# A gated delta-rule step: keys and queries against the state in one group, the squares summed on VectorE, and the Gram groups apart

## The reference

```
q = silu(conv(x @ Wq));  k, v likewise      # causal convolution over 4 tokens, w[0..3]
beta = sigmoid(x @ Wb)
q, k = l2norm(q), l2norm(k)                 # per head
M = I + strictly_lower(beta * k k^T);  u = M^-1 (beta v);  w = M^-1 (beta k)
for each chunk:   u = u - w S
                  o = q S + lower(q k^T) u
                  S = S + k^T u
x2 = x + layernorm(rmsnorm(o) @ Wo);  h = layernorm(x2)
out = x2 + layernorm(experts(h) + shared(h))    # router: 4 of 32 experts; shared: silu-gated pair of products
```

## Time and profile before

| | us |
|---|---|
| median of three runs | 1088.2 (1084.99, 1088.2, 1091.24) |
| the profiled execution | 1077.42, its span 1075.7 |
| busy in the span: PE, DVE, ACT | 862.9, 659.8, 340.2 |
| mean granted TensorE clock | 0.912 of full speed |

### The profile page before, as it was taken

One profiled execution on the slowest core, in us unless ns is written; L12 is line 12 of the kernel. 1 busy time (PEld: TensorE's weight loads), 2 busy tenths in 40 slices (PEclk: granted clock), 3 DMA queues, 4 the chain that ended last, 5 costly groups with the idle time before them and its releaser, 6 DMA issues. The chain is left out here.

```text
span 1075.7 us, 35367 instructions
## 1 busy us (share of the span) xinstructions
PE 862.9 (80%) x15631; PEld 655.3 (61%) x15632; DVE 659.8 (61%) x1251; ACT 340.2 (32%) x635; POOL 118.3 (11%) x187
## 2 busy tenths in 40 slices
PE   6585697898889999979988998388783899999900
PEld 5565666666567676656766767156452777887800
DVE  2788498688579778968967986943238122222226
ACT  2423423532443352343353344122321122122205
POOL 2000000000000000000000000000001445444244
PEclk9886698999899999999999999789896899999965
DMA  8110002005100200200200110020106699999768
GB/s 276 63 41 3 4 2 82 5 2 198 68 5 13 91 4 3 101 4 3 80 24 3 37 46 4 1 81 4 59 20 235 240 360 361 356 353 351 257 139 241
DMA packets 48641, 113.42 MB, mean 105 GB/s; under 512 B 8576, under 2 KB 8704, under 8 KB 48368
## 3 DMA queue, kind: packets, MB, share of 16 engines
q1 hardware_dynamic: 42224, 96.50, 24.7%
q0 software_dynamic: 6272, 14.68, 6.3%
HBM read 84.34 MB, written 26.84 MB: 103 GB/s over the span
## 5 line engine op out<-in xcount | busy, mean ns | idle before, releaser
L465 PE MATMUL bank<-xnT,wring 128*128 128x256 f32 x768 | 170.0, 382 | 0.0
L465 PEld LDWEIGHTS bank<-xnT,wring 128*128 128x128 f32 x768 | 145.6, 191 | 23.6 <-issue 4.2
L1575 PEld LDWEIGHTS ps_g<-xgT,wring 128*128 128x128 f32 x1024 | 120.8, 194 | 17.2 <-issue 17.2
L1575 PE MATMUL ps_g<-xgT,wring 128*128 128x128 f32 x1024 | 121.2, 277 | 1.3 <-ACT xgT L1605 1.3
L1708 DVE TENSOR_TENSOR hid<-ps_g,sg 128x160 f32<-128x160 f32 x32 | 10.4, 325 | 147.9 <-ACT sg L1615 147.9
L993 DVE SCALAR_TENSOR_TENSOR cv<-pre,taps,cv 128x1024 f32<-128x1024 f32 x72 | 92.4, 1283 | 2.1
L1484 POOL MEMSET xgT<- 128x512 f32 x2 | 1.0, 532 | 796.7 <-POOLq L1786 796.7
L608 PE MATMUL bank<-hT,sg_w 128*128 128x256 f32 x256 | 72.4, 410 | 0.0
L608 PE MATMUL bank<-hT,su_w 128*128 128x256 f32 x256 | 67.3, 399 | 0.0
L618 PE MATMUL bank<-sd_w,sh_h 128*128 128x512 f32 x128 | 66.5, 643 | 0.9 <-DVEq L1114 0.9
L1605 ACT ACTIVATE xgT<-ps_x 128x320 f32<-128x320 f32 x32 | 14.0, 437 | 160.0 <-PE ps_x L1564 160.0
(11 more groups left out here) (192 smaller groups left out, 1488.8 us busy)
## 6 DMA issues: line engine op xcount, KB each, us to landing
wring<-in_ffn_W_gate SPq DMA_DIRECT2D x32, 512.0 KB, 10.2
wring<-in_ffn_W_up SPq DMA_DIRECT2D x32, 512.0 KB, 11.1
wring<-in_ffn_W_down SPq DMA_DIRECT2D x32, 512.0 KB, 11.7
x_in<-in_attn_x SPq DMA_DIRECT2D x8, 512.0 KB, 3.5
x_res<-in_attn_x SPq DMA_DIRECT2D x8, 512.0 KB, 4.3
x_rows<-x SPq DMA_DIRECT2D x8, 512.0 KB, 2.8
h_rows<-h SPq DMA_DIRECT2D x8, 512.0 KB, 3.8
side_rows<-acc_sb SPq DMA_DIRECT2D x8, 512.0 KB, 6.0
```

The lines of the kernel that those rows point to most:

```text
L465: m = te.matmul(bank[:, c * COLS:(c + 1) * COLS], wqkv[:, w, kt, ct * P:(ct + 1) * P], xnT[:, kt, :], start=(kt == 0), stop=(kt == KT - 1))
L1575: m = te.matmul(ps_g[q % 2][:, (2 * a + i) * P:(2 * a + i + 1) * P], w[:, k, i * P:(i + 1) * P], xgT[q % 2][:, k, :], start=(k == 0), stop ...
```

## The change

Seven things are done at once:

- `core` multiplies the state with keys and queries in one group of 32 matmuls, each 32x64, into one bank (`ps_c[j % 2]`). The state is now the stationary operand, so the keys' product comes out turned, and `residual` turns it back with a transpose before it subtracts. The other products of a chunk go to the other bank, and the banks change roles from chunk to chunk. A chunk has four groups and four fillers.
- `output_squares` no longer multiplies q's squares by a second matrix. VectorE adds them, scaled, to the output's squares (`output_sums`), and four of eight matmuls a step remain.
- ScalarE's `take_projection` writes a second result, the bank times the last tap, into the convolution's output. VectorE's convolution starts from it with three taps.
- `turn_h` comes after the whole projection, and `take_h` after all of `take_projection`. The router moves into the first filler of the core.
- One Y moves a filler later, and so do E and D pieces.
- `gram` is split: groups 0 and 1 come between pieces of the up-projection ahead of the squares, 2 and 3 behind them; `take_x` comes ahead of `gate_factor`, and the ring's order has X ahead of F.
- On VectorE `scale_output` comes ahead of `turn_k` and `turn_v`, and `route_experts` stands between the two halves of `hidden`.

```diff
-ORDER = dict(... two="PHEFXIOGW", loop="PHVYEFXIOGW", ...)
+ORDER = dict(... two="PHEXFIOGW", loop="PHVYEXFIOGW", ...)
...
-    ps_ws, ps_o = banks[6], banks[7]
+    ps_c = banks[6:8]
...
-                    if n == 4 and phase not in ("begin", "one"):
-                        turn_h(s - 2, phase)
-            if phase not in ("begin", "one"):
-                router(s - 2, s + 1)
...
-                now = state[j % 2]
+                now, here, aside = state[j % 2], ps_c[j % 2], ps_c[(j + 1) % 2]
...
-                        m = te.matmul(ps_ws[quad(hh), i * DK:(i + 1) * DK], kq[quad(hh), i * J + j, 0, :], now[quad(hh), i, :], start=True, stop=True)
+                        m = te.matmul(here[quad(hh), i * 64:(i + 1) * 64], now[quad(hh), i, :], kq[quad(hh), i * J + j, :, :].rearrange("p a c -> p (a c)"),
+                                      start=(i == 0), stop=False, skip_group_check=True)
                 m.then_inc(ks_done, 1)
-                fill(5 * j)
...
+                fill(4 * j)
...
-                for i in range(I8):
-                    for hh in range(HT):
-                        te.matmul(ps_o[quad(hh), i * CH:(i + 1) * CH], now[quad(hh), i, :], kq[quad(hh), i * J + j, 1, :],
-                                  start=(i == 0), stop=False, skip_group_check=True)
-                fill(5 * j + 1)
...
+                if not (isinstance(s, int) and s == 0 and j == 0):
+                    pe.wait_ge(o_out, J * s + j)
+                    pe.sem_inc(pe_passed, 1)
                 pe.wait_ge(resid_ready, J * s + j + 1)
...
-            pe.wait_ge(qsq_ready, s + 1)
-            pe.wait_ge(osq_ready, s + 1)
+            pe.wait_ge(sums_ready, s + 1)
...
-                    te.matmul(bank[:, c * COLS:(c + 1) * COLS], headsq[:, :], q_sq[:, cols], start=True, stop=False)
-                    m = te.matmul(bank[:, c * COLS:(c + 1) * COLS], headsm[:, :], o_r[:, cols], start=False, stop=True)
+                    m = te.matmul(bank[:, c * COLS:(c + 1) * COLS], headsm[:, :], o_r[:, cols], start=True, stop=True)
...
-        FILL = ["VVVV", "Y", "Y", "Y", "Y", "E", "E", "E", "E", "", "D", "D", "D", "D", "F", "F", "F", "", "F", ""]
+        FILL = ["VVRVV", "Y", "Y", "Y", "YE", "E", "E", "E", "DD", "D", "D", "F", "F", "F", "F", ""]
...
         def body(s, phase):
             project(s, phase)
+            if phase != "one":
+                turn_h(s - 2, phase)
...
+            up(0)
+            up(1)
+            gram(s, phase, (0,))
+            up(2)
+            gram(s, phase, (1,))
+            up(3)
             output_squares(s - 1, phase)
-            if phase != "one":
-                for q in range(2, 4):
-                    shared_up(s - 2, phase, "F", 1, q)
-            gram(s, phase)
+            gram(s, phase, (2, 3))
             out_proj(s - 1, phase)
...
-                link(sc_e.activation(pre[:, w, 4 * half:4 * half + 4, HALO:], ring.bank(first, n)[:, :].rearrange("p (i t) -> p i t", t=TT), ACT.Copy))
+                bank = ring.bank(first, n)[:, :].rearrange("p (i t) -> p i t", t=TT)
+                sc_e.activation(pre[:, w, 4 * half:4 * half + 4, HALO:], bank, ACT.Copy)
+                link(sc_e.activation(cv[:, w, 4 * half:4 * half + 4, :], bank, ACT.Copy, scale=taps[:, w, TAPS - 1:TAPS]))
...
             take_projection(s, phase, 1, 0)
-            take_projection(s, phase, 2, 2, (0,))
+            take_projection(s, phase, 2, 2)
             if phase != "one":
                 take_h(s - 2, phase)
-            take_projection(s, phase, 2, 2, (1,))
-            if phase != "one":
                 take_scores(s - 2)
...
-            link(v.tensor_scalar(cv[:, w, :, :], pre[:, w, :, 0:TT], taps[:, w, 0:1], None, ALU.mult))
-            tap(w, 1)
+            tap(w, 0)
         def conv_end(w, s):
+            tap(w, 1)
             tap(w, 2)
-            tap(w, 3)
...
-            v.tensor_tensor(resid[:, :, :], ps_ws[:, 0:256].rearrange("p (i d) -> p i d", d=DK), v_tok[:, :, :].rearrange("p (i j) d -> p j i d", j=J)[:, j], ALU.subtract).then_inc(resid_ready, 1)
+            link(v.transpose(resid[:, :, :], ps_c[j % 2][:, :].rearrange("p (i a c) -> p i a c", a=2, c=CH)[:, :, 0, :]))
+            v.tensor_tensor(resid[:, :, :], resid[:, :, :], v_tok[:, :, :].rearrange("p (i j) d -> p j i d", j=J)[:, j], ALU.subtract).then_inc(resid_ready, 1)
...
+        def output_sums(s):
+            dve.wait_ge(qsq_ready, s + 1)
+            dve.wait_ge(osq_ready, s + 1)
+            v.scalar_tensor_tensor(out=o_r[:, :], in0=q_sq[:, :], scalar=RMS_EPS * DK * DK, in1=o_r[:, :], op0=ALU.mult, op1=ALU.add).then_inc(sums_ready, 1)
...
             silu_kq(1, 0, s)
+            output_sums(s - 1)
+            if phase != "one":
+                hidden_gate(s - 2, phase, 1)
+                route_experts(s - 2)
+                hidden_up(s - 2, phase, 1)
+            scale_output(s - 1)
             turn_k()
-            if phase != "one":
-                route_experts(s - 2)
             turn_v()
-            if phase != "one":
-                hidden(s - 2, phase, 1)
-            scale_output(s - 1)
             masks(s, phase)
```

More of the change, by code:

```diff
@@ L62 @@
 LAG = dict(P=0, G=0, X=-1, O=1, W=1, H=2, E=2, F=2, I=2, V=3, Y=3)
-ORDER = dict(begin="XPGX", one="PXOGW", two="PHEFXIOGW", loop="PHVYEFXIOGW", seven="PHVYEFIOGW", end="HVYEFIOWVYHEFIVY")
+ORDER = dict(begin="XPGX", one="PXOGW", two="PHEXFIOGW", loop="PHVYEXFIOGW", seven="PHVYEFIOGW", end="HVYEFIOWVYHEFIVY")
 LOOP_FROM, LOOP_TO = 3, STEPS - 1
@@ L239, in step_part @@
     sig_ready = [sem(f"sig_ready{n}") for n in range(3)]
-    act_ready = [sem(f"act_ready{n}") for n in range(3)]
+    v_turned = sem("v_turned")
     halo_done = sem("halo_done")
@@ L467, in project, with gram @@
                     m.then_inc(ring.full(first, n), 1)
-                    if n == 4 and phase not in ("begin", "one"):
-                        turn_h(s - 2, phase)
-            if phase not in ("begin", "one"):
-                router(s - 2, s + 1)
-        def gram(s, phase):
+        def gram(s, phase, columns=range(J)):
             first, st = where(phase, "G", s)
             pe.wait_ge(kq_ready, 2 * (s + 1))
-            for j in range(J):
+            for j in columns:
                 ring.wait_free(pe, first, st, j)
@@ L524, in core @@
                     for hh in range(HT):
-                        m = te.matmul(ps_ws[quad(hh), i * DK:(i + 1) * DK], invT[quad(hh), i * J + j, :], resid[quad(hh), i, :], start=True, stop=True)
+                        m = te.matmul(aside[quad(hh), i * DK:(i + 1) * DK], invT[quad(hh), i * J + j, :], resid[quad(hh), i, :], start=True, stop=True)
                 m.then_inc(solved, 1)
-                fill(5 * j + 2)
+                fill(4 * j + 1)
                 pe.wait_ge(unew_ready, J * s + j + 1)
@@ L532, in core @@
                     for hh in range(HT):
-                        m = te.matmul(ps_ws[quad(hh), i * DK:(i + 1) * DK], k_tok[quad(hh), i * J + j, :], unew[quad(hh), i, :], start=True, stop=True)
+                        m = te.matmul(aside[quad(hh), i * DK:(i + 1) * DK], k_tok[quad(hh), i * J + j, :], unew[quad(hh), i, :], start=True, stop=True)
                 m.then_inc(ds_done, 1)
-                fill(5 * j + 3)
+                fill(4 * j + 2)
                 pe.sem_inc(pe_passed, 1)
@@ L638, in fill @@
                 for c in FILL[n]:
+                    if c == "R":
+                        router(s - 2, STEPS if phase == "end" else s + 1)
+                        continue
                     at = done[c]
@@ L641, in fill @@
                     if c in "VY":
-                        if phase != "two" and not (phase == "end" and c == "V"):
+                        if phase != "two":
                             shared_down(s - 3, phase, "VY".index(c), at)
@@ L672, in _ @@
         turn_h(STEPS - 2, "end")
-        for ft in range(FT):
-            shared_down(STEPS - 3, "end", 0, ft)
-        router(STEPS - 2, STEPS)
         core(STEPS - 1, "end", filler(STEPS, "end"), STEPS, STEPS - 1)
-        for q in range(2):
+        for q in range(4):
             shared_up(STEPS - 2, "end", "F", 1, q)
         output_squares(STEPS - 1, "end")
-        for q in range(2, 4):
-            shared_up(STEPS - 2, "end", "F", 1, q)
         out_proj(STEPS - 1, "end")
@@ L1299, in _ @@
         route_experts(STEPS - 2)
+        output_sums(STEPS - 1)
         hidden(STEPS - 2, "end", 1)
```

54 lines of the change are left out of this document (27 added, 27 removed).

## The result

| | before | after |
|---|---|---|
| median of the timed runs, us | 1087.6 (1084.99 to 1091.24) | 1101.2 (1096.54 to 1102.49) |
| ratio, 95% interval | | 1.0131 (1.0100 to 1.0163) |
| span of the profiled execution | 1075.7 | 1099.5 |
| mean granted TensorE clock | 0.912 | 0.897 |

The change makes the kernel 1.3% slower. I had forecast 1086, no difference; the time lies at the upper end of the range and at rival 2 (1098). The profiled execution of before lies 1% under its median and that of after at its median, so the two spans overstate the difference (24 us against 14). I use them for where the time goes.

What follows compares the result with a forecast made beforehand. TensorE hardly rests and its instruction stream also limits it, with VectorE's slack 2.3 us. Terms over the eight steps sum to -8.4 us; +6 for the clock leaves -2.4, given as 1086 us against 1088.2, range 1072 to 1102.

Steps and rivals of the forecast that it cites:

- rival 2: Slower: turn_k and turn_v ahead of the masks delay h by 4.0 us, clock falls every step; about 1098, chance 0.24.
- The front: From turn_x's transposes to chunk 0's inverse product: 55.3 us, 2.1 later than now, on ScalarE's path by a hair.
- The core: From chunk 0's inverse product to the next step's turn_x: 33.0 us against 35.95 now.
- The late Y: In the core, the last Y behind the next chunk's group makes unew late: 2.0 us lost, with 0.4 before it.
- The clock's price: TensorE's granted clock falls after idle holes in about half of the steps: +6 us, bounds nothing to 15.
- The wide group: In each core chunk, one 32x64 group of 0.91 us replaces two of 0.68: 0.45 us saved a chunk.
- The issue stalls: TensorE stalls among small matmuls, some 127 pairs apart: fewer expected after the change, 1 us left in the core.
- The first core: The core without filler: 28.9 us at 960 instead of 1152 records, -5.5 us, above its chain of some 23.
- The sums: Query squares added on VectorE: output_sums costs 1.28 us there, TensorE saves four matmuls, 1.7 us a step.
- The stream: Dense small matmuls are limited to 3.8 to 4.2 us per 127 pairs; the core loses a fifth of its instructions.
- rival 3: Issue stalls don't depend on the number of instructions, or are hidden; about 1105, chance 0.04.
- the last: Last core, free of sigmoids: -5.4 us, with its front +3.7, together -1.7.

Runs made afterwards that it cites:

- e2: The changed kernel with the last tap as a VectorE multiply again and one ScalarE pass; ratio 1.0180 to the kernel before.
- e1: The changed kernel with VectorE's turn_k and turn_v ahead of scale_output again; ratio 1.0023 to the kernel before.
- e5: The changed kernel with the last Y moved back into chunk 0, behind its first filler; ratio 1.0057 to the kernel before.
- e4: The kernel before with only the one 32x64 group, the banks' roles and the residual's transpose; ratio 0.9740 to the kernel before.
- e3: The kernel before with only the squares' sums on VectorE, ahead of turn_k, and four matmuls fewer a step; ratio 1.0134.
- e12: The changed kernel with the query squares multiplied on TensorE again and output_sums gone; ratio 1.0306 to the kernel before.

## Why the prediction was wrong

**The front** was rightly read, and a little short. scale_output came at +12.0 (said +11.6), the inverse at +19.35 (+18.4), h at +45.7 (+44.8), the waits for it were 2.63 and 3.01 us (2 and 2.9), the core's entry at +56.5 (+55.3). ScalarE was the limit by a hair and VectorE just behind, as e2 shows. This is rival 2's mechanism, and e1 bears it out: in its step from 302.39 the core starts 2.5 us earlier, and the kernel gets 1.1% back.

**The core is the step that failed:** 37.2 us in place of 33.0, and 36.2 to 37.2 in all four full steps. The waits in it were rightly seen; the work and the stalls were put too low. By the rows of this core:

| core of the step from 402.36, us | forecast | measured |
|---|---|---|
| work | 27.5 | 31.2 |
| "issue" | 1 | 2.3 |
| waits for ScalarE or VectorE | 4.4 | 3.6 |
| core | 33.0 | 37.2 |

- The late Y was named, at 0.4 and 2.0 us of waiting, and the waits came (0.78 and 1.53). But e5 shows the core to be 3.7 us shorter without the move, because issue stalls, and in this step a fall of the clock, came with them.
- The clock's price, 6 us in all, I had put at the router, in half of the steps. In this step it held there (1.00 from 448 to 464) and fell in the core, and in the last full step both at the router (3.35 us at 642.39) and in the core (a filler of 2.08 us at 662.57). In the other two it fell behind the wait for h (the group at 357.16 takes 1.69 us, that at 543.52 takes 1.93), and the core still starts at +56.5 and +56.8: the router's wait, 1.5 us instead of 3.0, took it up. So the clock is the smaller part of the miss in the core: without a fall in it the work was 29.7 and 29.6 us, about 2.1 more than the sum had.
- The wide group: 0.91 us was to be the Gram groups' total without stalls. But 34.5 us in the earlier trace rows is busy time and holds no idle time, so it gives 1.08 us per 64 records. Start to start the group took 1.03, 1.36, 1.02 and 1.26 us in the four chunks; against eight groups of 0.68 that saves 0.8 us a step where 1.8 were counted. The three of them in this core are 0.9 of the missing work. What else makes the work longer no run shows.
- The issue stalls fell by 4.7 us a step, and that was right in kind.

The rule of rival 2 was that it decides if the inverse starts over 3 us later while the core falls by less than 2 us. It started 5.0 us later and the core rose by 1.2.

**The first core** was put at 28.9 us and took 33.0 (34.5 before). I had taken the longer of two limits, the stream at 3.8 us per 127 pairs and a chain of some 23 us. The rows show the stalls on top of the chain: 23.5 us and 11.0 of issue stalls before, 24.8 and 8.2 after. There are still four of some 2 us, one a chunk:

```profile
95.67 0.37 PE L530 MATMUL bank<-grams,unew 32*32 32x32 f32 x10 [2.00 <-issue]
...
104.24 0.37 PE L530 MATMUL bank<-grams,unew 32*32 32x32 f32 x11 [1.84 <-issue]
```

In e4, with the same instructions in the same core, they are 0.70, 0.18, 1.62 and 1.91, and that core takes 30.2. The same core takes 26.8 us in e1 and 28.4 in e5. Why the same stream stalls twice as long in the change no run here shows, nor whether it is the kernel or the one execution that was profiled.

**The sums** I had priced by their instruction (VectorE has time until the gate) and by the TensorE work saved. e3 and e12 show that neither is the price: what counts is which work stands behind the wait, and who needs its bank.

**The stream** as a limit, the argument against rival 3, held in the main: e4's 28 us come with fewer issue stalls (3.4 instead of 7.0 in the step, by the same sum as above). Rival 3 was not wholly off: the first core gave 1.5 us of the 5.5 counted, but the last gave 4.0 of 5.4 (35.6 us before, 31.6 after). I undervalued it, because I looked at it only together with the parts that take it back. The page of the Trainium skill that I named (Runtime: NRT & Kernel Launch, "Instruction fetch mechanics") has the fetch mostly hidden; here 7.0 us of an 89.1 us step were not.

**Chances.** Slower had 0.29, rival 2 alone 0.24. What should have moved them: VectorE's slack was 2.3 us and my own sum had the core start 2.1 late, so each further hair went straight to the end, while every saving in the core depended on ScalarE's order.

## What to carry to other kernels

Where three engines are within some 2 us of each other a step, price a moved instruction by what is queued behind its wait and which buffer that work frees, not by its own duration; the same 1.2 us instruction was worth +1.3, +0.4 or -1.7% by its place and what stood around it. When a change bundles one structural saving with re-orderings, build the saving alone in the old order first: here it was 2.6% faster, and the bundle 1.3% slower. When you fill a wait, look at the next wait downstream before you count the gain.

## What the runs showed of the hardware

- Inside dense groups of small matmuls TensorE stalls with nothing in the profile to release it. In the kernel before this "issue" time took 7.0 us of a step; with a fifth of the core's instructions gone (e4) it took 3.4 us. That it is the instruction stream is inferred, from the even distance of some 127 pairs and from e4; no run isolates it. The pages of before and after fit that: the queue of instructions moved 17 packets (of 16.4 KB) less with 4139 instructions less:

```profile
q8 instruction: 127, 2.08, 0.8%
...
q8 instruction: 110, 1.80, 0.7%
```

- Where the stalls fall, and how long they are, changes between profiled kernels with the same instructions in a core (8.2 us in the first core of after, 4.4 in that of e4, 2.2 in that of e1).
- The 32x64 form with the state as stationary operand takes 1.03 us for 32 matmuls (64 records) when nothing stalls, against 0.68 for the 32x32 form: 1.5 times for twice the columns.
- VectorE's transpose of 128x256 from PSUM takes 0.45 us, 0.49 start to start, as the prediction had it (0.45 and 0.5).
- The granted clock fell behind idle times of 3.01 us in two full steps of e1 and held behind the same 3.01 us in a third, at the same place of the same kernel. It fell in after behind 0.78 and 1.53 us, 3.3 us apart by their ends, and held in another of its steps behind the same two. The length of a hole alone does not say whether it will.
